# Two layers of a graph network: the gathered half of each node table first, and ScalarE scales the nodes' own part

## The chip, the cores and the metric

One core of a Trainium2 chip. The metric is the device time of one execution in microseconds (us), median of several. The core's engines run their own instruction streams in order and meet through semaphores: TensorE (PE, with PEld for its weight loads), VectorE (DVE), ScalarE (ACT), GpSimd (POOL) and SyncE (SP), which only starts transfers.

## The reference

6,250 nodes of 128 features, 106,250 edges sorted by destination. Two layers, each behind a layer norm and a ReLU, `h`, and each added to `x`:

```python
# layer 0: attention (GATv2)
xl, xr = h @ Wl + bl, h @ Wr + br
logits = leaky_relu(xl[src] + xr[dst] + edge_attr @ We, 0.2) @ att
out    = segment_sum(xl[src] * segment_softmax(logits, dst)[:, None], dst) + bias_out
x      = x + batch_norm(gelu(h + out))
# layer 1: messages, gated
em       = relu(layer_norm(concat(h[src], h[dst]) @ msg_w + msg_b)) * w[:, None]
messages = segment_mean(em, dst)
gate     = sigmoid(h @ gate_w + gate_b)
h_new    = relu(layer_norm(concat(h, messages) @ upd_w + upd_b))
x        = x + gate * h_new + (1 - gate) * h
```

## The kernel before

**Tiles.** A tile `t` is 125 nodes (50 tiles), a group `g` is four tiles (13 groups; the last has two). Edges lie in 64 chunks of 1,664 (13 x 128). A chunk's destinations fall in one or two windows of 125 nodes; a *pair* is a chunk and a window. There are 64 pairs, k = 0 to 63, worked in four blocks b of 4, 3, 3 and 3 tiles of 128 edges.

**Order.** Each layer goes through: layer norm statistics of the nodes, the *table stage*, the pair loop, and an end. The second layer has one more stage between table stage and pair loop, the *own part*.

**Table stage** (`tables` on TensorE and VectorE, `tables_of` on ScalarE). For each group: ScalarE normalises its rows (`norm_rows`, L1020, four instructions), TensorE turns them (`turn_rows`, L707), ScalarE copies them with ReLU into `feat_h` (`features`, L1014), TensorE multiplies each tile with the layer's 256 columns (`project`, L715: columns 0 to 127 give the row that edges gather by source, columns 128 to 255 the row by destination), VectorE adds the bias to either half (`add_bias`, L1321, two instructions: `rows`, a ring of three groups, and `dst_rows`, which stays on the chip). SyncE stores `rows` to `src_table` in DRAM (L493, two transfers a group); VectorE's writing of group g waits until the store of group g - 3 has landed. PSUM holds two groups (`rows_ps`, two banks each). In the first layer VectorE does other work between the groups (statistics, the list of the pairs). After the last group comes `raw_scale`: pair 0 is not gathered from the table, but from the inputs of the layer norm, so that GpSimd has it early; its rows go through norm, turn and product apart (`raw_norm`, `raw_turn`, `raw_features`, `raw_project`, `raw_rows`).

**Pair loop.** GpSimd gathers the 13 x 128 source rows of pair k into one of four buffers (`gather_pair`, L643, 13 indirect transfers). For k = 1 it first waits for the whole table (`tables_stored`). For k >= 4 each block waits until the buffer is free: in the first layer until the sums of pair k - 4 are made (`gat_sums`, L815), in the second until its messages are (`msg_message`, L888 and L892); and pair k waits for its records (`rec`), which SyncE loads in the second layer only after the messages of pair k - 4 (`feed`, L417). The engines work on a pair in a chain of stages with lags; in the second layer ScalarE makes the one-hot matrix (`one_hot`, L1206 and L1209) from `node_id` (L1555, VectorE), ahead of the pair's first product (L888).

**Own part** (second layer). For each group g: TensorE makes `feat_h` times the update's own columns and the gate's column (`update_own`, L936); ScalarE makes the gate (`gate_of`, L1224); VectorE makes `rest` = 1 - gate (L1757), `node_h` = max(node_h, 0) * rest (L1759), `node_x` += `node_h` (L1763), and then takes the product out of PSUM into `node_h` (L1765). PSUM again holds two groups:

```python
            def update_own(g):
                t0, t1 = GROUPS[g]
                pe.wait_ge(s_row, NGX + NG)
                ge(pe, s_zh, g - 1)
```

`s_zh` counts the groups whose L1765 is done, so the product of group g waits for the taking out of group g - 2. TensorE starts the pair loop once all 13 are taken out.

Of the kernel before, what the change touches and what calls it, by code (L numbers as in the profile page):

```python
# [15 lines left out]
D = 128  # L16
# [3 lines left out]
PP = 125  # L20
# [39 lines left out]
def gnn_layers(nc, a, out):  # L60
    with ExitStack() as ctx:
# [176 lines left out]

        rows_ps = [psum[:, (2 + 2 * u) * 512:(4 + 2 * u) * 512].rearrange("p (i f) -> p i f", i=GT) for u in range(2)]
# [41 lines left out]
        s_row = sem("s_row")  # L281
        s_src_out = [sem(f"s_src_out{u}") for u in range(3)]
# [87 lines left out]
        s_held = sem("s_held")  # L370
        s_zh = sem("s_zh")
# [329 lines left out]
        def turn_rows(pe, n, g):  # L701

            t0, t1 = GROUPS[g]
            pe.wait_ge(s_norm, n * NGX + g + 1)
            ge(pe, s_ht, n * NGX + g - 1 if g > 1 else 0)
            for t in range(t0, t1):
                i = nc.tensor.transpose(turn_ps[g % 2][:, t - t0, 0:PP], node_h[:, t, :], ident[0:PP, 0:PP])  # L707
            i.then_inc(s_tr, 1)

        def project(pe, n, g, weights):  # L710
            t0, t1 = GROUPS[g]
            pe.wait_ge(s_ht, n * NGX + g + 1)
            ge(pe, s_row, n * NGX + g - 1 if g > 1 else 0)
            for t in range(t0, t1):
                i = nc.tensor.matmul(rows_ps[g % 2][0:PP, t - t0, :], feat_h[:, t, :], weights[:, :], start=True, stop=True)  # L715
            i.then_inc(s_proj, 1)

# [8 lines left out]
        def tables(pe, n, weights):  # L726
            turn_rows(pe, n, 0)
            for g in range(NG):
                if g + 1 < NG:
                    turn_rows(pe, n, g + 1)  # L730
                project(pe, n, g, weights)
                if n == 0 and g == 6:
                    spread_chunks(pe)

# [7 lines left out]
        def raw_turn(pe, n, b):  # L742

            t0, t1 = BLK[b]
            pe.wait_ge(s_norm, raw_group(n, b) + 1)
# [14 lines left out]
        def _(pe):  # L760
# [170 lines left out]
            def update_own(g):  # L931
                t0, t1 = GROUPS[g]
                pe.wait_ge(s_row, NGX + NG)
# [65 lines left out]
        def _(act):  # L999
# [41 lines left out]
            def tables_of(n):  # L1041
# [7 lines left out]
                for g in range(NG):  # L1049
# [3 lines left out]
                    if ahead <= g + 2 < NG:  # L1053
                        norm_rows(n, g + 2)
# [171 lines left out]

            raw_deviations(1)
            for g in range(NG):
                gate_of(g)
                if g in RAW_NORM:  # L1230
                    raw_norm(1, RAW_NORM.index(g))
                if g in RAW_FEATURES:
                    raw_features(1, RAW_FEATURES.index(g))
            act.wait_ge(s_src_out[2], 2 * 32 * SLOT_GROUPS[2])
# [49 lines left out]
        def _(dve):  # L1284
# [27 lines left out]
            def add_bias(n, g, bias):  # L1312
# [6 lines left out]
                for h, to in enumerate((rows[0:PP, g % 3, 0:nt, :], dst_rows[:, t0:t1, :])):  # L1319
                    f = slice(h * D, (h + 1) * D)  # L1320
                    i = dve.tensor_tensor(to, rows_ps[g % 2][0:PP, 0:nt, f],  # L1321
                                          bias[0:PP, f].unsqueeze(1).to_broadcast([PP, nt, D]), ALU.add)
                i.then_inc(s_row, 1)
# [160 lines left out]
            raw_scale(0, gat)  # L1484
            rest_of_weights(0)
# [262 lines left out]
            layer_norm_scale(1, 1)  # L1748
            tables(1, msg_b, {})
            raw_scale(1, msg)  # L1750


            def own_part(g):
                t0, t1 = GROUPS[g]
                nt = t1 - t0
                dve.wait_ge(s_gate, g + 1)
                dve.tensor_scalar(rest[:, t0:t1], gate[:, t0:t1], -1.0, 1.0, ALU.mult, ALU.add).then_inc(s_rest, 1)  # L1757
                dve.wait_ge(s_rest, g + 1)
                dve.scalar_tensor_tensor(out=node_h[:, t0:t1, :], in0=node_h[:, t0:t1, :], scalar=0.0,  # L1759
                                         in1=rest[:, t0:t1].unsqueeze(2).to_broadcast([PP, nt, D]), op0=ALU.max,  # L1760
                                         op1=ALU.mult).then_inc(s_held, 1)
                dve.wait_ge(s_held, 2 * g + 1)
                dve.tensor_tensor(node_x[:, t0:t1, :], node_x[:, t0:t1, :], node_h[:, t0:t1, :], ALU.add).then_inc(s_held, 1)  # L1763
                dve.wait_ge(s_held, 2 * g + 2)
# [4 lines left out]
            for g in range(NG):  # L1769
                own_part(g)  # L1770
# [164 lines left out]
```

## Time and profile before

| | us |
|---|---|
| median of 3 runs (lowest, highest) | 2270.16 (2269.47, 2271.11) |
| the profiled execution: its time | 2270.79 |
| its span, first to last instruction | 2269.0 |
| busy: PE / PEld | 1644.5 / 1231.5 |
| busy: DVE / ACT / POOL | 1709.5 / 1232.5 / 1634.4 |
| mean granted TensorE clock | 0.902 |
| DMA | 83 GB/s, 189.19 MB |

Busy times are of one profiled execution; its time is 1.8 us more than its span. In the rows below, a timeline merges instructions of one line that follow each other: start in us, length in us, engine and line, what is written <- read, shapes, and how many; in brackets the idle time of the engine before it and what ended it ("issue": nothing that the profile shows). A float32 product is two MATMUL instructions, so a group of four tiles counts x8. A busy engine is not by itself the one that sets the end; which wait ends last in a stage has to be read there.

### The profile page before, as it was taken

To read this page: it belongs to the slowest core of one execution; us is meant where nothing else is said; L and a number is where in the kernel's file an instruction comes from. 1 tells how busy PE (TensorE), PEld (TensorE's weight loads), DVE (VectorE), ACT (ScalarE), POOL (GpSimd) and SP (SyncE) were. 2 spreads that over 40 slices of the span, in tenths; PEclk is the share of its full clock that TensorE was granted. 3 is DMA by queue.
4 is the path that set the end of the run, shared out by engine and by line. 5 is a ranking of instruction groups with operands and counts; after the bars stand their busy time and mean duration, and the time that the engine had idled before them with its cause. 6 is when DMAs were issued, how large, how long until landed. Compare 5 with 4: busy or idle time off the path is not lost.

```text
span 2269.0 us, 43295 instructions
## 1 busy us (share of the span) xinstructions
PE 1644.5 (72%) x9256; PEld 1231.5 (54%) x9256; DVE 1709.5 (75%) x6093; ACT 1232.5 (54%) x3996; POOL 1634.4 (72%) x1742
## 2 busy tenths in 40 slices
PE   5488887777778777877776767767766776666666
PEld 4265555555545555555565555555655655555454
DVE  6787777676777777777768777778778778777777
ACT  5344444444434444444556666667666666566655
POOL 5777777777777777777137777777777777777774
PEclk9799999999999999999978888888888888898988
DMA  9433333333333333332242332332333333323322
GB/s 190 100 86 86 86 78 84 86 77 84 78 86 77 82 81 84 77 83 72 54 114 66 85 83 78 84 84 76 83 84 76 83 85 80 79 76 83 76 68 62
DMA packets 176752, 189.19 MB, mean 83 GB/s; under 512 B 100940, under 2 KB 132708, under 8 KB 176564
## 3 DMA queue, kind: packets, MB, share of 16 engines
q0 software_dynamic: 54192, 111.40, 20.0%
q1 hardware_dynamic: 120965, 75.89, 13.1%
q10 hardware_dynamic: 1472, 0.73, 0.2%
q14 instruction: 103, 0.84, 0.1%
q8 instruction: 20, 0.33, 0.1%
HBM read 172.91 MB, written 14.97 MB: 83 GB/s over the span
## 4 chain that ended last, share of the span: by engine, by line
POOL 31%; issue 18%; PE 14%; DVE 12%; ACT 10%; DMA 3%; DVEq 2%; POOLq 1%; ACTq 0%
POOL room L643 31%; PE psum L888 4%; ACT room L1206 4%; PE psum L892 3%; DVE room L1818 3%; DMA room<-src_table,rec 3%; ACT room L1209 2%; PE psum L815 2%; ACT rows L1186 2%; ACT room L1198 1%; PE psum L715 1%; PE psum L797 1%; DVE room L1804 1%; DVEq L1535 1%; DVE dfar L1561 1%
## 5 line engine op out<-in xcount | busy, mean ns | idle before, releaser
L643 POOL DMA_INDIRECT room<-src_table,rec x1638 | 1564.7, 955 | 519.1 <-issue 482.1
L888 PE MATMUL psum<-room,ident 128*128 128x384 f32 (+1 forms) x512 | 286.0, 645 | 295.7 <-ACT room L1209 207.0
L1186 ACT ACTIVATE rows<-psum 128x128 f32<-128x128 f32 x832 | 216.9, 271 | 318.3 <-DVE room L1804 318.3
L892 PEld LDWEIGHTS psum<-room 125*128 125x128 f32 x1664 | 277.0, 230 | 112.5 <-issue 64.1
L815 PE MATMUL psum<-room 128*125 128x128 f32 x1664 | 255.9, 294 | 85.8 <-ACT room L1136 81.9
L1118 ACT ACTIVATE room<-psum 128x384 f32<-128x384 f32 (+1 forms) x256 | 130.4, 509 | 289.6 <-PE psum L787 281.6
L815 PEld LDWEIGHTS psum<-room 128*125 128x125 f32 x1664 | 210.3, 195 | 136.6 <-ACT room L1136 135.5
L1599 DVE TENSOR_TENSOR room<-psum,room 128x384 f32<-128x384 f32 (+1 forms) x256 | 150.9, 590 | 173.4 <-ACT room L1118 88.5
L892 PE MATMUL psum<-room 125*128 125x128 f32 x1664 | 273.4, 312 | 0.0
L888 PEld LDWEIGHTS psum<-room,ident 128*128 128x128 f32 x512 | 92.1, 225 | 315.2 <-ACT room L1209 167.0
L1804 DVE TENSOR_TENSOR room<-psum,msg_g 128x384 f32<-128x384 f32 (+1 forms) x256 | 150.2, 587 | 149.9 <-PE psum L892 149.9
L905 PE MATMUL psum<-room 128*125 128x128 f32 x1664 | 249.8, 293 | 13.5 <-ACT room L1198 11.9
L1818 DVE SCALAR_TENSOR_TENSOR room<-room,rstd_e,msg_beta 128x128 f32<-128x128 f32 x832 | 244.1, 351 | 10.2
L905 PEld LDWEIGHTS psum<-room 128*125 128x125 f32 x1664 | 226.5, 207 | 20.2 <-issue 16.1
L797 PE MATMUL psum<-room,natt 128*125 128x384 f32 (+1 forms) x512 | 231.4, 535 | 6.3 <-DVE room L1599 6.1
L787 PE MATMUL psum<-ident,room 128*128 128x128 f32 x832 | 143.8, 287 | 118.9 <-DMA room<-src_table,rec 117.8
L1794 DVE TENSOR_SCALAR room<-nfree,rec 128x125 f32<-128x125 f32 x832 | 227.4, 367 | 0.1
L1127 ACT ACTIVATE room<-room,nloc 125x384 f32<-125x384 f32 (+1 forms) x256 | 163.8, 640 | 91.1 <-DVE nloc L1614 88.1
L787 PEld LDWEIGHTS psum<-ident,room 128*128 128x128 f32 x832 | 100.3, 144 | 185.5 <-DMA room<-src_table,rec 170.6
L780 PE MATMUL psum<-room 128*128 128x384 bf16 (+1 forms) x768 | 182.3, 348 | 21.1 <-DVE room L1591 21.1
L1186 ACT ACTIVATION_READ_ACCUMULATOR rows<-psum 128x1 f32 x832 | 168.9, 203 | 0.0
L805 PEld LDWEIGHTS psum<-ident,room 125*128 125x128 f32 x832 | 110.5, 146 | 103.0 <-issue 72.1
(250 smaller groups left out, 2650.6 us busy)
## 6 DMA issues: line engine op xcount, KB each, us to landing
room<-dst_perm SPq DMA_DIRECT2D x128, 416.0 KB
room<-src_table,rec POOLq DMA_INDIRECT x1638
src_table<-rows SPq DMA_DIRECT2D x24, 224.0 KB
node_x<-in_x SPq DMA_DIRECT2D x5, 560.0 KB
x_rows<-node_x SPq DMA_DIRECT2D x12, 224.0 KB
out_rows<-node_x SPq DMA_DIRECT2D x12, 224.0 KB
rec<-rec_rows SPq DMA_DIRECT2D x125, 19.5 KB
pair_info<-pair_list SPq DMA_DIRECT2D x128, 2.0 KB
```

The costliest lines, as they stand in the source:

```text
L643: pool.indirect_dma_start(out=xg[:, u, t * P:(t + 1) * P], out_offset=None, in_=table[:, :], in_offset=bass.IndirectOffsetOnAxis(ap=rec[:, ...
L780: nc.tensor.matmul(m_bank[c][:, cols], dws[:, v, p, :], oht[:, v, t0 * P:t1 * P], start=(p == 0), stop=False, skip_group_check=True)
L787: i = nc.tensor.matmul(m_bank[c][:, j * P:(j + 1) * P], xg[:, u, t * P:(t + 1) * P], ident[:, :], start=False, stop=(t == t1 - 1), is_tran ...
L797: nc.tensor.matmul(logit_bank[c][0:W, cols], natt[:, :], act_m[:, c, cols], start=True, stop=True).then_inc(s.logit, 1)
L815: i = nc.tensor.matmul(sum_bank[u % 2][0:W, 0:D], prob[:, c, t - t0, 0:W], xg[:, u, t * P:(t + 1) * P], start=(t == 0), stop=(t == T - 1), ...
L888: nc.tensor.matmul(msg_bank[b][:, cols], ident[:, :], xg[:, u, t0 * P:t1 * P], start=True, stop=False, skip_group_check=True)
L892: i = nc.tensor.matmul(msg_bank[b][:, j * P:(j + 1) * P], msg_oht[0:W, v, t * P:(t + 1) * P], dwin[0:W, v, :], start=False, stop=(t == t1 ...
L905: i = nc.tensor.matmul(sum_bank[u % 2][0:W, 0:D], pm[:, u % 2, t, 0:W], zr[:, b, j * P:(j + 1) * P], start=(t == 0), stop=(t == T - 1), sk ...
L1186: i = nc.scalar.activation(sq[:, j * P:(j + 1) * P], msg_bank[b][:, j * P:(j + 1) * P], ACT.Square, accum_out=var_e[:, c, j:j + 1])
L1794: i = dve.tensor_scalar(pm[:, v, t, 0:W], nfree[:, v, :], rec[:, u, T + t:T + t + 1], rec[:, u, 2 * T + t:2 * T + t + 1], ALU.is_equal, AL ...
L1804: dve.tensor_tensor(hgs[:, c, 0:nt * P].rearrange("p (j f) -> p j f", f=D), msg_bank[b][:, 0:nt * P].rearrange("p (j f) -> p j f", f=D), m ...
L1818: i = dve.scalar_tensor_tensor(out=xz[:, c, j * P:(j + 1) * P], in0=hgs[:, c, j * P:(j + 1) * P], scalar=rstd_e[:, c, j:j + 1], in1=msg_be ...
```

## The change

*Tables.* The product of a tile is made in two passes of 128 columns. `project` makes the gathered half for all 13 groups first, into four half-size places in PSUM (`half_ps`), and VectorE's `add_bias` writes only `rows`. A new pass over the groups, `project_near` on TensorE and `near_rows` on VectorE, makes `dst_rows`; on VectorE it stands behind `raw_scale`, on TensorE ahead of `raw_turn` (first layer) and of `update_own` (second). In the second layer VectorE normalises groups 9 to 12 (14 instructions) in ScalarE's place.

*Own part.* VectorE's L1759 goes. ScalarE multiplies instead (`kept`, one instruction for each tile, ReLU with `rest` as scale), for group g - 1 right behind the gate of group g. VectorE makes `rest` of group g ahead of the rest of its work on group g - 1.

```diff
         def project(pe, n, g, weights):
             t0, t1 = GROUPS[g]
             pe.wait_ge(s_ht, n * NGX + g + 1)
-            ge(pe, s_row, n * NGX + g - 1 if g > 1 else 0)
+            ge(pe, s_row, n * NGX + g - 3 if g > 3 else 0)
+            if n == 1 and g < 4:
+                pe.wait_ge(s_near_row, NG)
             for t in range(t0, t1):
-                i = nc.tensor.matmul(rows_ps[g % 2][0:PP, t - t0, :], feat_h[:, t, :], weights[:, :], start=True, stop=True)
+                i = nc.tensor.matmul(half_ps[g % 4][0:PP, t - t0, :], feat_h[:, t, :], weights[:, 0:D], start=True, stop=True)
             i.then_inc(s_proj, 1)
+
+        def project_near(pe, n, g, weights):
+            t0, t1 = GROUPS[g]
+            if g < 4:
+                pe.wait_ge(s_row, n * NGX + NG + g - 3)
+            else:
+                pe.wait_ge(s_near_row, n * NG + g - 3)
+            for t in range(t0, t1):
+                i = nc.tensor.matmul(half_ps[(NG + g) % 4][0:PP, t - t0, :], feat_h[:, t, :], weights[:, D:2 * D], start=True, stop=True)
+            i.then_inc(s_near_proj, 1)
...
             def update_own(g):
                 t0, t1 = GROUPS[g]
-                pe.wait_ge(s_row, NGX + NG)
+                pe.wait_ge(s_near_row, 2 * NG)
                 ge(pe, s_zh, g - 1)
...
-                    if ahead <= g + 2 < NG:
+                    if ahead <= g + 2 < NG and (n == 0 or g + 2 not in NORM_DVE):
                         norm_rows(n, g + 2)
...
+            def kept(g):
+                act.wait_ge(s_rest, g + 1)
+                for t in range(*GROUPS[g]):
+                    i = nc.scalar.activation(node_h[:, t, :], node_h[:, t, :], ACT.Relu, scale=rest[:, t:t + 1])
+                i.then_inc(s_kept, 1)
+
             raw_deviations(1)
             for g in range(NG):
                 gate_of(g)
+                if g > 0:
+                    kept(g - 1)
                 if g in RAW_NORM:
                     raw_norm(1, RAW_NORM.index(g))
                 if g in RAW_FEATURES:
                     raw_features(1, RAW_FEATURES.index(g))
+            kept(NG - 1)
...
+            def near_rows(n, bias):
+
+                for g, (t0, t1) in enumerate(GROUPS):
+                    nt = t1 - t0
+                    dve.wait_ge(s_near_proj, n * NG + g + 1)
+                    dve.tensor_tensor(dst_rows[:, t0:t1, :], half_ps[(NG + g) % 4][0:PP, 0:nt, :],
+                                      bias[0:PP, D:2 * D].unsqueeze(1).to_broadcast([PP, nt, D]), ALU.add).then_inc(s_near_row, 1)
...
             layer_norm_scale(1, 1)
+            dve.wait_ge(s_norm_scale, PART0[1] + 2)
+            for g in NORM_DVE:
+                for t in range(*GROUPS[g]):
+                    i = dve.tensor_scalar(node_h[:, t, :], node_x[:, t, :], rstd[:, t:t + 1], nmr[:, t:t + 1], ALU.mult, ALU.add)
+                i.then_inc(s_norm_dve, 1)
             tables(1, msg_b, {})
             raw_scale(1, msg)
+            near_rows(1, msg_b)
...
+            def rest_of(g):
+                t0, t1 = GROUPS[g]
                 dve.wait_ge(s_gate, g + 1)
                 dve.tensor_scalar(rest[:, t0:t1], gate[:, t0:t1], -1.0, 1.0, ALU.mult, ALU.add).then_inc(s_rest, 1)
-                dve.wait_ge(s_rest, g + 1)
-                dve.scalar_tensor_tensor(out=node_h[:, t0:t1, :], in0=node_h[:, t0:t1, :], scalar=0.0,
-                                         in1=rest[:, t0:t1].unsqueeze(2).to_broadcast([PP, nt, D]), op0=ALU.max,
-                                         op1=ALU.mult).then_inc(s_held, 1)
-                dve.wait_ge(s_held, 2 * g + 1)
+
+            def own_part(g):
+                t0, t1 = GROUPS[g]
+                nt = t1 - t0
+                dve.wait_ge(s_kept, g + 1)
                 dve.tensor_tensor(node_x[:, t0:t1, :], node_x[:, t0:t1, :], node_h[:, t0:t1, :], ALU.add).then_inc(s_held, 1)
-                dve.wait_ge(s_held, 2 * g + 2)
+                dve.wait_ge(s_held, g + 1)
                 dve.tensor_tensor(node_h[:, t0:t1, :], rows_ps[g % 2][0:PP, 0:nt, 0:D],
                                   upd_b[0:PP, :].unsqueeze(1).to_broadcast([PP, nt, D]), ALU.add).then_inc(s_zh, 1)
 
             dve.wait_ge(s_x1_out, NG * 32)
-            for g in range(NG):
-                own_part(g)
+            for g in range(NG + 1):
+                if g < NG:
+                    rest_of(g)
+                if g > 0:
+                    own_part(g - 1)
                 if g in RAW_ROWS:
                     raw_rows(1, RAW_ROWS.index(g), msg_b)
```

## Rows read from the trace of the kernel before

**Rows 1.** page, costliest groups: busy us, mean ns, idle before and releaser

```profile
L643 POOL DMA_INDIRECT room<-src_table,rec x1638 | 1564.7, 955 | 519.1 <-issue 482.1
```

**Rows 2.** line 643 from 1250 to 2230 us: idle before it, us and times

```profile
  issue: 226.7, 744
  PE psum L892: 6.7, 22
```

**Rows 3.** line 888 from 1219 to 1900 us: idle before it, us and times

```profile
  DMA room<-src_table,rec: 0.6, 1
```

**Rows 4.** line 888 from 1900 to 2215 us, the same

```profile
  DMA room<-src_table,rec: 100.0, 52
```

**Rows 5.** GpSimd's timeline: start, length (us), line, [idle before <-releaser]

```profile
62.47 3.88 POOL L643 DMA_INDIRECT room<-src_table,rec  x1 [3.31 <-DMA src_table<-rows]
...
115.02 0.94 POOL L643 DMA_INDIRECT room<-src_table,rec  x1 [0.30 <-issue]
...
1181.14 0.94 POOL L643 DMA_INDIRECT room<-src_table,rec  x1 [17.25 <-DMA src_table<-rows]
...
1230.41 0.96 POOL L643 DMA_INDIRECT room<-src_table,rec  x1 [0.30 <-DMA rec<-rec_rows]
...
1234.21 0.94 POOL L643 DMA_INDIRECT room<-src_table,rec  x1 [0.30 <-issue]
```

**Rows 6.** TensorE's timeline at the first pairs of either layer

```profile
112.50 1.14 PE L815 MATMUL psum<-room 128*125 128x128 f32 x8 [0.78 <-ACT room L1136]
...
1219.29 2.07 PE L888 MATMUL psum<-room,ident 128*128 128x512 f32 x2 [7.80 <-ACT room L1209]
```

**Rows 7.** SyncE's timeline: the records of pairs 4 and 5, second layer

```profile
1228.22 0.39 SPq L417 DMA_DIRECT2D rec<-rec_rows  x1
...
1244.94 0.38 SPq L417 DMA_DIRECT2D rec<-rec_rows  x1
```

**Rows 8.** VectorE's timeline in the first layer's tables

```profile
33.99 0.69 DVE L1321 TENSOR_TENSOR rows<-psum,b_lr 125x512 f32<-125x512 f32 x1 [3.49 <-DMA src_table<-rows]
34.60 0.68 DVE L1321 TENSOR_TENSOR dst_rows<-psum,b_lr 125x512 f32<-125x512 f32 x1
...
57.06 0.41 DVE L1321 TENSOR_TENSOR rows<-psum,b_lr 125x256 f32<-125x256 f32 x1
...
61.82 0.17 DVE L1341 SCALAR_TENSOR_TENSOR raw_nmr<-raw_nmr,raw_rstd 128x13 f32<-128x13 f32 x1
```

**Rows 9.** timelines, second layer's tables: ScalarE, TensorE, VectorE

```profile
1155.49 1.64 ACT L1020 ACTIVATE node_h<-node_x,nmr,rstd 125x128 f32<-125x128 f32 x4
...
1159.13 1.89 PE L715 MATMUL psum<-msg_wc,feat_room 128*125 128x256 f32 x8
...
1177.16 0.41 DVE L1321 TENSOR_TENSOR rows<-psum,msg_b 125x256 f32<-125x256 f32 x1
```

**Rows 10.** timelines in the own-part stage, TensorE, ScalarE, VectorE

```profile
1188.04 2.05 PE L936 MATMUL psum<-upd_w,feat_room 128*125 128x129 f32 x8 [0.20 <-DVE node_h L1765]
...
1192.93 1.12 PE L936 MATMUL psum<-upd_w,feat_room 128*125 128x129 f32 x8 [1.15 <-DVE node_h L1765]
...
1190.13 0.26 ACT L1224 ACTIVATE gate<-psum,gate_b 125x4 f32<-125x4 f32 x1 [1.99 <-PE psum L936]
...
1192.89 0.69 DVE L1759 SCALAR_TENSOR_TENSOR node_h<-node_h,rest 125x512 f32<-125x512 f32 x1
1193.62 0.69 DVE L1763 TENSOR_TENSOR node_x<-node_x,node_h 125x512 f32<-125x512 f32 x1
1194.34 0.69 DVE L1765 TENSOR_TENSOR node_h<-psum,upd_b 125x512 f32<-125x512 f32 x1
...
1214.93 0.16 DVE L1555 TENSOR_TENSOR node_id<-turned,iota_p 128x1 f32<-128x1 f32 x1
```

**Rows 11.** stretches: busy us (count) by engine, granted clock, DMA share, GB/s

```profile
1183.00:1190.00 7.00, 4.02 (x17) 3.78 (x18) 6.12 (x12) 2.13 (x7) 5.48 (x6) 0.56 0.18 45
1190.00:1200.00 10.00, 7.56 (x60) 6.91 (x59) 9.59 (x18) 5.62 (x16) 7.87 (x8) 0.97 0.16 44
```

More of the change, by code:

```diff
@@ L237, in z_bank @@
             return banks[2 + g % NZ][0:PP, :].rearrange("p (i f) -> p i f", i=GT)
+        half_ps = [banks[2 + u].rearrange("p (i f) -> p i f", i=GT) for u in range(4)]
         rows_ps = [psum[:, (2 + 2 * u) * 512:(4 + 2 * u) * 512].rearrange("p (i f) -> p i f", i=GT) for u in range(2)]
@@ L281, in gnn_layers @@
         s_row = sem("s_row")
+        s_near_proj = sem("s_near_proj")
+        s_near_row = sem("s_near_row")
+        s_norm_dve = sem("s_norm_dve")
+        NORM_DVE = (9, 10, 11, 12)
         s_src_out = [sem(f"s_src_out{u}") for u in range(3)]
@@ L703, in turn_rows @@
             t0, t1 = GROUPS[g]
-            pe.wait_ge(s_norm, n * NGX + g + 1)
+            if n == 1 and g in NORM_DVE:
+                pe.wait_ge(s_norm_dve, NORM_DVE.index(g) + 1)
+            else:
+                pe.wait_ge(s_norm, n * NGX + g + 1)
             ge(pe, s_ht, n * NGX + g - 1 if g > 1 else 0)
@@ L733, in tables @@
                     spread_chunks(pe)
+            for g in range(NG):
+                project_near(pe, n, g, weights)
         RAW_NORM, RAW_TURN, RAW_FEATURES, RAW_PROJECT, RAW_ROWS = (range(i, i + 2 * NB, 2) for i in (1, 3, 4, 5, 6))
@@ L744, in raw_turn @@
             t0, t1 = BLK[b]
-            pe.wait_ge(s_norm, raw_group(n, b) + 1)
+            pe.wait_ge(s_norm, raw_group(n, b) + 1 - (len(NORM_DVE) if n == 1 else 0))
             for t in range(t0, t1):
@@ L1318, in add_bias @@
                 ge(dve, s_src_out[g % 3], 32 * (n * SLOT_GROUPS[g % 3] + g // 3))
[L1319 to L1323, printed above, removed]
+                dve.tensor_tensor(rows[0:PP, g % 3, 0:nt, :], half_ps[g % 4][0:PP, 0:nt, :],
+                                  bias[0:PP, 0:D].unsqueeze(1).to_broadcast([PP, nt, D]), ALU.add).then_inc(s_row, 1)
+            def near_rows(n, bias):
[4 more added lines that the diff above has]
+                                      bias[0:PP, D:2 * D].unsqueeze(1).to_broadcast([PP, nt, D]), ALU.add).then_inc(s_near_row, 1)
             def raw_scale(n, s):
@@ L1748, in _ @@
             layer_norm_scale(1, 1)
+            dve.wait_ge(s_norm_scale, PART0[1] + 2)
[3 more added lines that the diff above has]
+                i.then_inc(s_norm_dve, 1)
             tables(1, msg_b, {})
             raw_scale(1, msg)
+            near_rows(1, msg_b)
+            def rest_of(g):
+                t0, t1 = GROUPS[g]
+                dve.wait_ge(s_gate, g + 1)
+                dve.tensor_scalar(rest[:, t0:t1], gate[:, t0:t1], -1.0, 1.0, ALU.mult, ALU.add).then_inc(s_rest, 1)
             def own_part(g):
```

5 lines of the change are left out of this document (3 added, 2 removed).

## Prediction, made before the changed kernel ran

> **What bounds the kernel now.** I read the page's costliest groups first. GpSimd's gathers [rows 1] take 955 ns each and stand 0.3 us apart, so 13 of them, one pair, take 16.3 us, and 63 pairs fill 1,025 us of each layer. The waits of that line [rows 2] then show that in the second layer's loop it waits for nothing but its own issue: 226.7 us in 744 waits are issue, 6.7 us in 22 end with TensorE, at the same 0.3 us each. So in both loops the gathers are one unbroken run, and the end comes as much later as the gathers of pair 4 and later come later. Whether the engines or GpSimd lead has to be asked apart. TensorE's first product of a block waits 0.6 us for gathered rows up to 1900 us, and 100.0 us after it [rows 3, 4]: in the second layer the engines start far behind the gathers, catch up about 1 us a pair and then live on them. A late start of the engines therefore counts only through what it does to GpSimd, if it is made up by the end.
>
> Next come GpSimd's timeline and what releases it [rows 5 to 7]. Pairs 1 to 3 need the stored table: the run starts at 62.47 and at 1181.14. Pair 4 is the 40th gather, at 115.02 and at 1234.21, and needs a buffer or records that only the engines' work on pair 0 frees. In the first layer TensorE's first sums of pair 0 end at 112.50 + 1.14 = 113.64; the gather comes at 115.02, so the slack is 1.3 us. In the second the records of pair 4 are asked for at 1228.22, after pair 0's messages, and have landed by 1230.41 (2.2 us): slack 3.8 us. Those of pair 5, asked for at 1244.94, land at 1247.1, and its gather is due 16.4 us after 1234.21, at 1250.6: slack 3.5 us. Thus a table stored earlier gives at most these slacks, 1.3 and 3.5 us, and a start of the engines later than they allow is paid in full.
>
> **Tables, first layer.** VectorE's two halves of a group stand at 33.99 and 34.60 [rows 8]: 0.6 us each, so taking out 12.5 of them spares 7.5 us before the last table row. Not all of it comes through: the row of 33.99 waited 3.49 us for the store of three groups earlier to land. Such landings stay where they are while the transfers of the opening run, and a faster VectorE only waits longer. I take 1.8 us of the 7.5 (bounds 0 and 7.5). The table is then stored some 2.7 us sooner, which pair 1 gets. The half rows come back behind `raw_scale`, in front of everything that VectorE still does before pair 0. VectorE alone would need 7.5 us. TensorE must make them too, out of four places: four groups are ready, the fifth can start when the first is taken out. A product of eight instructions of 128 columns takes 1.14 us, about 0.98 us from one to the next [rows 6]; after a pause it takes 2.05 [rows 10]. That is 0.6 + 8 x 0.98 + 0.5 + 0.4 = 9.3 us, or 11.4 with two slow groups; I take 10.4. From the last row to the end of `raw_scale`, 57.06 to 61.99, 0.3 us of the other half goes. So pair 0 starts 10.4 - 1.8 - 0.3 = 8.3 us later, its first sums end at 121.9, and the gather of pair 4 moves from 115.02 to 122.0: **+7.0 us** (likely 4 to 9; bounds -1.3, if all 7.5 us come through and TensorE keeps up, and +10).
>
> **Tables, second layer.** Before, ScalarE's four norms of a group take 1.64 us and a copy about 0.5, and TensorE's 256 columns 1.89 with a turn beside them [rows 9]: a group about every 2.1 us from either. Now TensorE needs 0.98 and about 0.43 for the turn, and ScalarE has norms for four groups fewer. VectorE's 14 norms, at most 0.38 us each, lie in its wait for the first products. The last row, at 1177.16 before, I put at 1170.3 (VectorE writes one half at 0.6 us; stores of three groups need to land within 4.2 us). `raw_scale` takes 4.3 us, then the other half 9.4 us with TensorE quick: 1184.0. The first gate is ready at 1184.1 + 1.12 + 0.3 = 1185.5.
>
> **Own part.** Here the order of waits matters more than the work. Before, a group cost VectorE three instructions about 0.7 us apart (1192.89, 1193.62, 1194.34) and a short one, some 2.25 us, with everything else beside it; ScalarE waited 1.99 us before a gate [rows 10]. Now ScalarE's stream reads: gate of g, multiplication of g - 1, gate of g + 1. The gate of g + 1 needs TensorE's product, which needs a free half of PSUM, which needs VectorE's taking out of g - 1, which needs the multiplication of g - 1 that has only just ended. No step of this ring overlaps another, although two groups fit in PSUM. One turn [rows 9, 10]: gate to multiplication 0.16; four instructions 1.64; to VectorE 0.06; addition 0.73; taking out 0.69; to TensorE 0.15; product 1.12, or 2.05 at the lower clock; to ScalarE 0.04. Sum 4.59 or 5.52 us. The product is slow where the granted clock averages 0.56 and quick where it is 0.97 [rows 11]; TensorE was busy 4.02 of 7 us in the one and 7.56 of 10 in the other. In the ring it works 1.1 to 2.0 us a turn, and as much again in every second turn on pair 0's rows, so it will be now on one level, now on the other: 5.1 us.
>
> The first multiplication ends at 1188.1, eleven turns later it is 1244.2; the half group, VectorE's last two takings out and the node numbers bring `node_id` to 1247.3, against 1215.09. The engines start pair 0 **32.2 us** later (26.6 to 36.9 by the two levels). Of pair 0's raw rows, ScalarE's norms and copies, TensorE's turns and products and VectorE's additions lie in the ring's waits and cost nothing. What the removed L1759 gives, 13 x 0.7 = 9 us of VectorE, is worth nothing, for VectorE waits in the ring.
>
> SyncE is queued behind it: the records of pair 4 are asked for after pair 0's messages. So GpSimd, done with pairs 1 to 3 some 53 us after its start near 1173.5, stands idle from about 1227 to 1263. With the slack of pair 5 the run moves by 32.2 - 3.5 = **+28.7 us** (23.1 to 33.4). The engines' own lag grows by only 3.5 us, which at 1 us a pair is made up before the last 15 pairs.
>
> **Sum.** 7.0 + 28.7 = 35.7 us on a span of 2269.0 gives 2304.7; its own time 2270.79 becomes 2306.5. The median lies 0.6 below that time: 2306.
>
> **Two rules.** ScalarE's four instructions take 1.64 us [rows 9], 410 ns each. The Trainium skill (VectorE: DVE Perf Modes, the section on the TRN2 errata) gives ScalarE 224 cycles and one a column at 1.2 GHz, and says that many small tiles pay the fixed part each time; 50 instructions where VectorE had 13 are what it warns of. Its figure is 293 ns; by it, as an estimate, a turn is 0.47 us shorter and the sum 2301. The trace's row decides here.
>
> The quick and slow product are the rows' two levels, 2.4 and 1.2 GHz. The Trainium skill (TensorE: Matmul & The Clock Gate, What's actually happening) calls the lower one the default that activity lifts; taken at its word, a TensorE busy a quarter to a third of each turn stays low, a turn is 5.52 us and the sum about 2311. That TensorE is on the lower level throughout is the last case below.
>
> **Rivals.**
> *The ring isn't closed; ScalarE is the bound.* If the multiplication of g - 1 were covered by a product already made, ScalarE's work would count: 13 gates of 0.16, 50 x 0.41, 13 x 0.41 for the raw norms, 2 us of copies: 30 us from 1185.5, `node_id` at about 1217.5. That is 2.4 us later, inside the slack of 3.5; only the first layer's 7.0 is left: 2276. ScalarE's 1.99 us waits speak for room; `update_own`'s unchanged wait speaks against it.
> *Faster: the start of the gathers decides.* If VectorE's relief (0.7 of 2.25 us a group) shortened the own part, to node numbers before 1215, GpSimd would gain up to the 3.5 us of the second layer, and with the first layer's halves hidden 1.3 there: 2266. It decides from a turn under 2.2 us and under 1.3 us of added wait before pair 0. Against it stand the ring and a VectorE with no pause between `raw_scale` and pair 0.
> *TensorE on the lower level throughout.* Turns of 5.52 us add 4.7; nearly all second-half groups at 2.05 us delay the own part by a further 9: 2320. For it speaks TensorE's short share of a turn; against it 0.97 in a stretch with waits of 1.15 us.
>
> **How the numbers follow.** Forecast 0.84, ScalarE bound 0.06, faster 0.04, lower level throughout 0.06. The forecast's own range is 2297 to 2315, from 4 and 23.1 up to 9 and 33.4 with a little for pair 0's start. It holds some nine tenths of its case; half of the slow case and the forecast's edges bring the range 2293 to 2319 to 8 in 10. About 0.2%, 4.5 us, is what a measurement of this kernel can tell from no change. Within it falls a part of the second case: 0.02; faster 0.04; slower 0.94.
>
> **What would show it.** Gates (L1224) about 5 us apart, each of ScalarE's waits ended by L936 and each of VectorE's by ScalarE's multiplication. GpSimd idle some 37 us before pair 4 of the second layer, the wait ended by the records, and 7 us before pair 4 of the first, ended by L815. The table stored earlier in both layers, about 2.7 and 7 us. Gates 2.3 to 2.6 us apart would make me wrong; so would gathers of pair 4 that don't follow the engines.

## The result and the profile after

The changed kernel takes **2309.8 us** (median of 4, 2307.9 to 2310.6), the kernel before 2270.4 beside it: ratio 1.0171 (1.0159 to 1.0183), 1.7% slower. Forecast were 2306 and a range of 2293 to 2319. The profiled execution has a span of 2308.8 us, 39.8 more than before, at a mean granted clock of 0.893.

The gathers' line of the page, and GpSimd's timeline at the points of [rows 1, 5]:

```profile
L649 POOL DMA_INDIRECT room<-src_table,rec x1638 | 1559.5, 952 | 570.6 <-issue 480.0
```

```profile
61.77 0.99 POOL L649 DMA_INDIRECT room<-src_table,rec  x1 [10.01 <-DMA src_table<-rows]
...
125.38 0.94 POOL L649 DMA_INDIRECT room<-src_table,rec  x1 [7.73 <-PE psum L838]
...
1183.75 0.94 POOL L649 DMA_INDIRECT room<-src_table,rec  x1 [8.39 <-DMA src_table<-rows]
...
1271.96 0.94 POOL L649 DMA_INDIRECT room<-src_table,rec  x1 [39.44 <-DMA rec<-rec_rows]
...
1290.82 1.07 POOL L649 DMA_INDIRECT room<-src_table,rec  x1 [2.93 <-DMA rec<-rec_rows]
```

The idle time before the gathers grew by 51.5 us in all; the part put down to issue did not grow (482.1 us before, 480.0 now). Two waits that [rows 5] don't have set the time: 7.73 us ahead of pair 4 in the first layer, ended by TensorE's sums, and 39.44 in the second, ended by the records. Pair 4 moved from 115.02 to 125.38, **+10.4 us**, and from 1234.21 to 1271.96; the last gather of the kernel starts 39.8 us later than before. So the second layer has **+29.5**. Its table is stored at 1183.75, 7.8 us sooner within the layer (1181.14 + 10.4 - 1183.75), and that gains nothing: GpSimd only waits longer ahead of pair 4.

Behind the two waits, TensorE's and SyncE's timelines (they answer to [rows 6, 7]):

```profile
123.46 1.14 PE L838 MATMUL psum<-room 128*125 128x128 f32 x8 [0.78 <-ACT room L1159]
...
1260.77 2.07 PE L911 MATMUL psum<-room,ident 128*128 128x512 f32 x2 [9.05 <-ACT room L1232]
```

```profile
1269.13 0.39 SPq L423 DMA_DIRECT2D rec<-rec_rows  x1
...
1287.51 0.38 SPq L423 DMA_DIRECT2D rec<-rec_rows  x1
```

The sums come 10.96 us later, the records of pair 4 are asked for 40.9 us later. VectorE's timeline in the first layer's tables ([rows 8]); L1351 writes table rows, L1359 the near rows:

```profile
34.16 0.69 DVE L1351 TENSOR_TENSOR rows<-psum,b_lr 125x512 f32<-125x512 f32 x1 [3.17 <-DMA src_table<-rows]
...
49.07 0.69 DVE L1351 TENSOR_TENSOR rows<-psum,b_lr 125x512 f32<-125x512 f32 x1 [4.32 <-DMA src_table<-rows]
...
58.30 0.43 DVE L1351 TENSOR_TENSOR rows<-psum,b_lr 125x256 f32<-125x256 f32 x1 [1.71 <-DMA src_table<-rows]
...
62.75 0.17 DVE L1378 SCALAR_TENSOR_TENSOR raw_nmr<-raw_nmr,raw_rstd 128x13 f32<-128x13 f32 x1
62.84 2.48 DVE L1359 TENSOR_TENSOR dst_rows<-psum,b_lr 125x512 f32<-125x512 f32 x4
...
72.50 1.02 DVE L1359 TENSOR_TENSOR dst_rows<-psum,b_lr 125x512 f32<-125x512 f32 x2 [0.18 <-PE psum L736]
```

The view by tile says how long VectorE waited, from 20 to 66 us, before it could write `rows` (us, times). In the trace of the kernel before this line reads 5.5, 3:

```profile
  DMA src_table<-rows: 13.3, 5
```

VectorE was relieved of 7.5 us between the table's rows and waited 7.8 us more for stores to land. The last row is written at 58.30, no sooner than before (57.06). Then the near rows take 10.7 us, with TensorE the slower of the two at the end (0.18 us before each).

One turn of the own part, all engines but GpSimd and the transfers ([rows 10]):

```profile
1207.54 0.26 ACT L1247 ACTIVATE gate<-psum,gate_b 125x4 f32<-125x4 f32 x1 [3.69 <-PE psum L959]
1207.70 1.27 ACT L1253 ACTIVATE node_h<-node_h,rest 125x128 f32<-125x128 f32 x4
1207.83 0.17 DVE L1800 TENSOR_SCALAR rest<-gate 125x4 f32<-125x4 f32 x1 [2.54 <-ACT gate L1247]
...
1209.00 0.69 DVE L1806 TENSOR_TENSOR node_x<-node_x,node_h 125x512 f32<-125x512 f32 x1 [0.99 <-ACT node_h L1253]
1209.72 0.69 DVE L1808 TENSOR_TENSOR node_h<-psum,upd_b 125x512 f32<-125x512 f32 x1
...
1210.56 2.05 PE L959 MATMUL psum<-upd_w,feat_room 128*125 128x129 f32 x8 [2.21 <-DVE node_h L1808]
1212.65 0.26 ACT L1247 ACTIVATE gate<-psum,gate_b 125x4 f32<-125x4 f32 x1 [2.54 <-PE psum L959]
```

The ring is there as the prediction drew it: gate, multiplication, addition, taking out, product, gate, each released by the one before, 5.11 us a turn. All 13 gates together waited 43.9 us for the product (the view of line 1247), and TensorE's granted clock over these turns (window, columns as in [rows 11]) was nearly at the lower level:

```profile
  PE psum L959: 43.9, 13
```

```profile
1200.00:1250.00 50.00, 27.93 (x119) 25.25 (x119) 17.02 (x34) 19.58 (x64) 24.90 (x26) 0.54 0.14 36
```

### The profile page after: what moved, and what is told of

Its sections match the earlier page's. It is cut to its first block, busy times and chain, and to the rows that moved or that the text cites. A ratio compares the mean times of both kernels' runs of the same rounds, so it can differ in the third digit from the quotient of the medians.

```text
span 2308.8 us, 43732 instructions
## 1 busy us (share of the span) xinstructions
PE 1661.4 (72%) x9456; PEld 1259.5 (55%) x9456; DVE 1709.2 (74%) x6094; ACT 1240.4 (54%) x4032; POOL 1629.2 (71%) x1742
## 4 chain that ended last, share of the span: by engine, by line
POOL 32%; issue 19%; PE 14%; DVE 12%; ACT 10%; DMA 3%; DVEq 2%; POOLq 1%; ACTq 0%; SPq 0%
POOL room L649 32%; PE psum L911 4%; ACT room L1229 3%; PE psum L915 3%; DVE room L1864 3%; DMA room<-src_table,rec 3%; PE psum L838 2%; ACT room L1232 2%; ACT rows L1209 1%; PE psum L820 1%; PE psum L959 1%; PE psum L810 1%; DVEq L1573 1%; ACT room L1221 1%; DVE room L1850 1%
## 5 line engine op out<-in xcount | busy, mean ns | idle before, releaser
L649 POOL DMA_INDIRECT room<-src_table,rec x1638 | 1559.5, 952 | 570.6 <-issue 480.0
```

What stands on the lines that cost most here:

```text
L649: pool.indirect_dma_start(out=xg[:, u, t * P:(t + 1) * P], out_offset=None, in_=table[:, :], in_offset=bass.IndirectOffsetOnAxis(ap=rec[:, ...
```

## The experiments

The first four kernels ran on one chip beside the kernel before, which took 2271.0 us there. In each experiment's diff, `...` stands for lines left out.

**One half of the change each.** `tables_only` has the changed table stages and the own part of before. Its diff against the changed kernel:

```diff
             for g in range(NG):
                 gate_of(g)
-                if g > 0:
-                    kept(g - 1)
...
-                dve.wait_ge(s_kept, g + 1)
+                dve.wait_ge(s_gate, g + 1)
+                dve.tensor_scalar(rest[:, t0:t1], gate[:, t0:t1], -1.0, 1.0, ALU.mult, ALU.add).then_inc(s_rest, 1)
+                dve.wait_ge(s_rest, g + 1)
+                dve.scalar_tensor_tensor(out=node_h[:, t0:t1, :], in0=node_h[:, t0:t1, :], scalar=0.0,
+                                         in1=rest[:, t0:t1].unsqueeze(2).to_broadcast([PP, nt, D]), op0=ALU.max,
+                                         op1=ALU.mult).then_inc(s_held, 1)
+                dve.wait_ge(s_held, 2 * g + 1)
...
```

> The changed table stages in both layers with the own part of before. If the ring in the own part is what costs the second layer 29 us: pair 4 of the first layer stays where the changed kernel has it (125.4 us, 10.4 later than before), the own part takes 31 to 32 us from its first gate again, and of the second layer's delay only 0 to 1.5 us is left: a span of 2279 to 2281. If instead the second layer's added wait before the own part (near rows behind the scale) is itself a large part of the 29 us, the span is 2285 or more. If the earlier table of the second layer is worth something by itself, the span is 2276 or less.

`own_only` is the kernel before with `rest_of`, `kept` and the shorter `own_part` of the change.

> The table stages of before with the own part as changed. The ring theory: gates 5.1 us apart, node numbers about 27 us later than before (1242), gathers of pair 4 and 5 of the second layer 24 to 26 us later, pair 4 of the first layer at 115.0 as before, a span of 2293 to 2296. The rival, that ring and tables only cost so much together (TensorE left cold by the tables, for instance), puts the turn under 4.5 us and the span under 2290.

Measured: tables only 2278.7 us, ratio 1.0031 (1.0020 to 1.0042); own part only 2298.6, ratio 1.0119 (1.0102 to 1.0136). Thus +7.7 and +27.6, together 35.3 of the 39.4 that the whole costs. The tables' span, 2277.9 us, is 1.1 below what was expected, and that of the own part, 2298.1, is 2.1 above; gates stand 5.11 us apart with the own part alone, so the ring needs no help from the tables. Pair 4's gather in the second layer, with the tables alone (L649) and with the own part alone (L644):

```profile
1241.08 0.94 POOL L649 DMA_INDIRECT room<-src_table,rec  x1 [6.06 <-DMA rec<-rec_rows]
```

```profile
1259.34 0.95 POOL L644 DMA_INDIRECT room<-src_table,rec  x1 [27.66 <-DMA rec<-rec_rows]
```

With the tables alone, pair 4 of the first layer is 8.6 us late, and within the second layer it is 1.7 us *early*. That does not last: pair 5 then waits 2.92 us for its own records and starts 9.4 us late (1259.99), so that 0.9 us of the delay is the second layer's. With the own part alone the first layer is as before, and the wait in the second is ended by the same records.

**Opening the ring by order alone.** The changed kernel with two pairs of calls exchanged, so that ScalarE's multiplication of g - 1 stands ahead of the gate of g, and VectorE's addition and taking out of g - 1 ahead of `rest` of g. No work changes.

```diff
             for g in range(NG):
-                gate_of(g)
                 if g > 0:
                     kept(g - 1)
+                gate_of(g)
...
-                if g < NG:
-                    rest_of(g)
                 if g > 0:
                     own_part(g - 1)
+                if g < NG:
+                    rest_of(g)
```

> The changed kernel with the same instructions in another order: ScalarE multiplies group g - 1 ahead of the gate of g, and VectorE finishes group g - 1 ahead of the subtraction of g. If the closed ring is the cost, a turn falls from 5.11 to about 3.0 us (addition 0.73, taking out 0.69, subtraction 0.27, multiplication 1.26 and the ways between), node numbers come about 17 us earlier, at 1239, and the span is about 2292 (2289 to 2296). If the amount of ScalarE's work or the fixed part of its 50 instructions is the cost, nothing moves: 2307 to 2310.

Measured 2284.0 us, ratio 1.0056 (1.0039 to 1.0073): 25.9 us faster than the changed kernel. Its span, 2282.7 us, lies 6.3 below the expected range. Its timeline:

```profile
1207.34 1.28 ACT L1253 ACTIVATE node_h<-node_h,rest 125x128 f32<-125x128 f32 x4 [0.77 <-DVE rest L1800]
1207.37 1.11 PE L959 MATMUL psum<-upd_w,feat_room 128*125 128x129 f32 x8 [1.59 <-DVE node_h L1808]
...
1208.53 0.26 ACT L1247 ACTIVATE gate<-psum,gate_b 125x4 f32<-125x4 f32 x1
1208.65 0.69 DVE L1806 TENSOR_TENSOR node_x<-node_x,node_h 125x512 f32<-125x512 f32 x1 [1.35 <-ACT node_h L1253]
...
1209.37 0.69 DVE L1808 TENSOR_TENSOR node_h<-psum,upd_b 125x512 f32<-125x512 f32 x1
1209.98 0.17 DVE L1800 TENSOR_SCALAR rest<-gate 125x4 f32<-125x4 f32 x1
1210.18 1.28 ACT L1253 ACTIVATE node_h<-node_h,rest 125x128 f32<-125x128 f32 x4 [0.24 <-DVE rest L1800]
```

Product and gate have left the ring: they start and end beside the multiplication. What is left is multiplication, addition, taking out, `rest`: 2.85 us a turn, still above the 2.25 of before [rows 10]. A quick product alone can't account for this gain: `filler`, the next run, has it in the closed ring and gains 10.8 us. The order of the calls was the large price. That of the multiplications' new place is small: this kernel is 5.3 us slower than the one with the changed tables alone. The expectation had the turn nearly right, at 3.0 us, and its sum wrong: twelve turns that are 2.1 us shorter make 25 us, not 17. The node numbers are ready at 1232.24, 24.2 us sooner than in the changed kernel; 2.4 of these are the first layer's, whose pair 4 starts at 122.95.

**The clock's part.** The changed kernel with dummy products in the turns of groups 1 to 11 (nine a turn, or four where TensorE has pair 0's raw product to make), into a free bank, so that TensorE doesn't rest in the ring:

```diff
+                if 0 < g < NG - 1:
+                    for _ in range(4 if g in RAW_PROJECT else 9):
+                        nc.tensor.matmul(banks[7 if g < 8 else 0][0:PP, 0:D], feat_h[:, g, :], upd_w[:, 0:D], start=True, stop=True)
```

> The changed kernel with products that nobody reads behind each group's product in the own part (nine tiles, four where pair 0's rows are made), into banks that are free then: they only keep TensorE busy in its wait. If the lower clock is the 0.94 us by which the turn stands above 4.2 us, the product takes 1.1 in place of 2.06 us in about ten turns and the span falls by 8 to 11 us, to about 2299. If the clock does not follow TensorE's own load, the product stays at 2.06 us and the span at 2308 or above.

Measured 2299.0 us, ratio 1.0124 (1.0107 to 1.0141). More work for TensorE took 10.8 us off. In its window the granted clock is 1.00 for 0.54, TensorE is busy 30.4 of 40 us for 27.9 of 50, and the product takes 1.11 us; gates stand 4.18 us apart in place of 5.11:

```profile
1200.00:1240.00 40.00, 30.38 (x258) 28.73 (x256) 16.04 (x32) 19.33 (x63) 27.54 (x27) 1.00 0.18 46
```

```profile
1212.14 1.11 PE L959 MATMUL psum<-upd_w,feat_room 128*125 128x129 f32 x8 [1.09 <-DVE node_h L1811]
...
1213.29 0.26 ACT L1250 ACTIVATE gate<-psum,gate_b 125x4 f32<-125x4 f32 x1 [2.27 <-PE psum L959]
```

The last gather starts 11.6 us sooner than in the changed kernel. Some 9.7 of these are the own part (node numbers at 1246.73 for 1256.41); about as much as is left, 1.7, is that the records of pair 5 are asked for 16.7 us after those of pair 4 and not 18.4.

**The tables of the second layer alone**, all else as before (a kernel beside it ran 2271.0, as for the next three):

> The tables of the second layer alone are built as the change builds them; the first layer's tables and the whole own part stay as before. The run with both layers' tables changed and the own part as before came out 7.7 us over the kernel before, and the fourth pair's gather of its first layer 8.6 us later. Theory A: all of that is the first layer's, where the near rows (10.6 us) stand on the path; in the second layer the messages' node rows are asked for some 2.8 us later, which the slack of about 3.5 us hides, and the earlier table store is hidden as well: 2270 to 2272 us, the same. Theory B: the near rows cost in the second layer too: 2273 us or more. Theory C: the table stored 7.6 us sooner lets GpSimd start sooner and that reaches the end: 2265 us or less.

Measured 2270.6 us, ratio 1.0000 (0.9991 to 1.0009): theory A. The 7.7 us of `tables_only` are the first layer's, to within the 1 us or so that a median can tell. The node numbers are ready some 2.4 us later within the layer, which is hidden; the table stored 6.1 us sooner within the layer gains nothing either.

**A fourth buffer for the table's rows.** The changed kernel with `rows` and its semaphores four deep:

```diff
-        rows = sb("rows", [P, 3, GT, D])
+        rows = sb("rows", [P, 4, GT, D])
...
-                ge(dve, s_src_out[g % 3], 32 * (n * SLOT_GROUPS[g % 3] + g // 3))
+                ge(dve, s_src_out[g % 4], 32 * (n * SLOT_GROUPS[g % 4] + g // 4))
...
```

> The changed kernel with four buffers for the table rows in place of three (and one semaphore fewer elsewhere). VectorE's 13.3 us of waits for stored rows in the first layer should fall to under half. Theory A (the waits for landings took what the removed near rows gave): the last row of the table is written some 4 to 6 us sooner, the near rows follow, and the time falls by as much: 2304 to 2307 us. Theory B (the stores themselves are the limit, and the wait moves on to them): the table is stored no sooner, but the near rows still start earlier, because VectorE runs ahead of the stores by one group more: 2306 to 2308 us. Theory C (the near rows don't stand on the path): 2309 to 2311 us.

Measured 2302.9 us, ratio 1.0135 (1.0120 to 1.0150), 6.9 less than the changed kernel. Lines by tile and by GpSimd's timeline:

```profile
  DMA src_table<-rows: 9.1, 5
```

```profile
119.56 0.95 POOL L648 DMA_INDIRECT room<-src_table,rec  x1 [7.37 <-PE psum L837]
```

The last row is written at 52.93 (58.30 with three buffers) and pair 4 starts 5.8 us sooner: theory A, 1.1 us below its range. Landings had taken what the removed near rows gave, and the fourth buffer does not give all of it back. The wait did not fall under half: two thirds of it remained. And beside the kernel before with four buffers (`before_four`, below), whose last row stands at 53.96 and whose VectorE never waits for a landing there, the near rows taken from between bring the last row 1.0 us forward, not 7.5.

**Putting the multiplication elsewhere.** If VectorE shall be relieved in the own part, the multiplication and the addition can be one instruction a tile there. ScalarE's norms already end in a ReLU, so the maximum can go. On the kernel before:

```diff
-                dve.scalar_tensor_tensor(out=node_h[:, t0:t1, :], in0=node_h[:, t0:t1, :], scalar=0.0,
-                                         in1=rest[:, t0:t1].unsqueeze(2).to_broadcast([PP, nt, D]), op0=ALU.max,
-                                         op1=ALU.mult).then_inc(s_held, 1)
-                dve.wait_ge(s_held, 2 * g + 1)
-                dve.tensor_tensor(node_x[:, t0:t1, :], node_x[:, t0:t1, :], node_h[:, t0:t1, :], ALU.add).then_inc(s_held, 1)
+                for t in range(t0, t1):
+                    i = dve.scalar_tensor_tensor(out=node_x[:, t, :], in0=node_h[:, t, :], scalar=rest[:, t:t + 1],
+                                                 in1=node_x[:, t, :], op0=ALU.mult, op1=ALU.add)
+                i.then_inc(s_held, 1)
...
```

First with the second layer's tables as changed (the four groups that VectorE normalises there get their ReLU by an instruction of their own), and then with two groups of its near rows moved up between far ones:

> The second layer's tables as in the change, the first layer as before, and the own part wholly on VectorE, with the multiplication by one less the gate and the addition of the nodes in one instruction per column tile (node_h * rest + node_x), no maximum, and the ReLU of VectorE's four norms put between the rows of the table. A group of the own part should take about 1.95 us on VectorE in place of 2.25, over 12.5 groups 3.8 us less; the nodes' rows are then asked for about 1 us sooner than before the change. Theory A: 2265 to 2268 us. Theory B (the path in the second layer is not VectorE's but the table's store and the gathers): 2269 to 2272 us.

> As the kernel with the fused own part, but the near rows of the first two groups are written between the far rows of groups 5, 6 and after, so that 1.4 us less of them stands behind the table. Theory A: 1 to 2 us faster than that kernel, 2263 to 2267 us. Theory B (the waits for stored rows take the room): the same as that kernel within 1 us.

Measured 2268.3 us for either, ratios 0.9984 (0.9975 to 0.9992) and 0.9987 (0.9978 to 0.9995): the first is 0.3 us above its theory A, and the moved near rows gave nothing that shows, its theory B. Then by itself, and with the fourth buffer (before beside these three: 2270.0):

> The kernel before with only the own part fused on VectorE (node_h * rest + node_x in one instruction per column tile; the maximum goes). A group should take some 0.3 us less, 3.8 us over the second layer. Theory A (in the kernel before, the store of the second layer's table holds GpSimd as long as the node side does): 2269.5 to 2271.5 us, the same, and the fused own part needs the table stored sooner to be worth anything. Theory B (the node side holds it): 2266 to 2268 us.

> The kernel before the change with four buffers for the table rows in place of three. Its VectorE waits 5.5 us in the first layer for stored rows; in the changed kernel the fourth buffer took 4.2 us off such waits (13.3 to 9.1) and 6.9 us off the time. Theory A (landings hold the first layer back here too, if less): 1.5 to 4 us faster, 2267 to 2269.5 us. Theory B (here VectorE's near rows fill the waits, so nothing is gained): 2270 to 2272 us.

> The kernel with the second layer's tables of the change, the fused own part on VectorE and the first two near rows between far rows (2268.3 us), with four buffers for the table rows. Theory A (the gain of the fourth buffer is the first layer's and adds to it): 2264 to 2267 us, below both kernels by 0.2% or more. Theory B: no further gain, 2268 to 2270 us.

Measured: fused own part alone 2267.0 (0.9983, 0.9974 to 0.9992), fourth buffer alone 2266.7 (0.9983, 0.9974 to 0.9992; VectorE's 5.5 us of waits for stores in the first layer are gone), all together **2259.4** (0.9951, 0.9937 to 0.9964), 0.5% faster than the kernel before and 2.2% faster than the changed one. The first fits its theory B by its number, the second is 0.3 us below its theory A. The third is 4.6 us faster than its theory A: the fourth buffer, expected to help the first layer alone, takes 3.2 us off there (pair 4 at 111.07 for 114.31 in `second_fused_two`), and in the second layer's tables a last wait of 1.5 us for a landing goes and the node numbers come 2.2 us sooner within the layer.

The fused own part gained 3 us where theory A of its expectation said nothing, and not for theory B's reason either. GpSimd's timeline in that kernel:

```profile
1182.54 0.94 POOL L643 DMA_INDIRECT room<-src_table,rec  x1 [16.77 <-DMA src_table<-rows]
...
1231.47 0.94 POOL L643 DMA_INDIRECT room<-src_table,rec  x1 [0.30 <-issue]
```

Pair 4 follows pair 3 without a wait, as before [rows 5]: the node side did not hold it. But the 39 gathers of pairs 1 to 3 took 48.9 us, and 53.1 before (1181.14 to 1234.21). The last section shows where they gained it.

**The fused own part and the fourth buffer, without any part of the change.**

> The kernel before with the fused own part and four buffers for the table rows, and no part of the change. Each alone measured 0.9983 of the kernel before (2267.0 and 2266.7 us against 2270.0); the kernel that has both, and the second layer's tables of the change too, measured 0.9951 (2259.4 us). Theory A (GpSimd's start is then the limit of the second layer, and only the table stored first makes use of the faster own part): the two gains don't add up, 2263.5 to 2267 us. Theory B (the second layer's tables as changed give nothing): 2258 to 2261 us.

Measured 2262.7 us, ratio 0.9963 (0.9949 to 0.9977; before 2271.3). It lies beneath theory A's range by 0.8 us and above theory B's by 1.7, so it decides for neither; its interval overlaps that of the kernel that has the second layer's tables too (0.9937 to 0.9964). Their traces differ: here pair 4 starts at 1227.42 right behind pair 3, there at 1223.18 after a wait for records, and the last gathers start at 2207.46 and 2203.32. Two lines of the kernel with those tables:

```profile
1170.16 0.94 POOL L648 DMA_INDIRECT room<-src_table,rec  x1 [9.41 <-DMA src_table<-rows]
...
1223.18 0.99 POOL L648 DMA_INDIRECT room<-src_table,rec  x1 [4.29 <-DMA rec<-rec_rows]
```

Whether the second layer's tables are worth these 3 to 4 us once both sides of the own part are faster stays open at this precision.

## Why the prediction was right

**The mechanism** held in its main steps: the two waits, what ended them, the ring, GpSimd's idle time (39.4 and 7.7 us; said were some 37 and 7), and in the second layer a table that is stored sooner for nothing. Sizes in it did not, as the terms below show. `order` shows that the cause of the large term is the closed ring: with the same instructions, 25.9 us go. The three rivals fall. ScalarE as the bound wants gates that wait for nothing, and they waited 43.9 us. A faster end wants turns under 2.2 us. The lower clock level was nearly true of the ring, but its 2320 needs two more things that did not come: slow near rows (from 1190 to 1200 us the granted clock was 1.00) and multiplications of 1.64 us.

**The sum** was 35.7 us for a measured 39.8 of span, each term by itself:

*First layer, +7.0 forecast, +10.4 in the trace after* (+10.3 in `filler`, +8.6 in `tables_only`, +7.9 in `order`, which have the same tables). The near rows took 10.7 us for 10.4. What failed is "I take 1.8 us of the 7.5": of VectorE's relief nothing came through here, -1.2 us; in the other three traces the last row stands at 57.2, 55.5 and 56.1, which is -0.2, 1.5 and 1.0 us. The waits for landings and the `four_buffers` run show that the stores took most of it. In the trace after, the first layer's table is stored 0.7 us sooner and not 2.7. The lower bound, 0 of 7.5, was nearer to their mean than the 1.8. The slack of 1.3 us was mis-sized as well: the gather of pair 4 started 0.78 us after the sums had ended (124.60 to 125.38), and pair 0's 10.96 us became 10.36, so 0.6 us of slack was there.

*Turn of the ring, 5.1 us forecast, 5.11 measured.* This is luck: two errors that cancel. The four multiplications were priced by the norms, 1.64 us [rows 9], and took 1.26; one alone is 0.39 us, so the step from one to the next is (1.26 - 0.39) / 3 = 0.29 us. The 293 ns that the prediction drew from the Trainium skill (VectorE: DVE Perf Modes, the section on the TRN2 errata) was the right one, and the row of the norms the wrong neighbour: those read a scale and a bias per partition, these a scale only (which of these makes the difference was not tried). And the product was taken as now quick, now slow; from 1200 on it took 2.05 or 2.06 us in nine of ten full groups and 1.11 in one, whose turn is 4.17 us. `filler` puts the price on the second: 0.94 us a turn. With the right multiplication and the mixed clock a turn would have been 0.38 us shorter and the sum some 4.6 us less, about 2301, too low. The Trainium skill's rule on the clock (TensorE: Matmul & The Clock Gate, What's actually happening), taken at its word, had the right level for the ring, and this trace agrees there: 0.54 in the window above.

*Start of the ring.* The last table row was put at 1170.3 and stands at 1179.87, which is 1169.5 once the first layer's 10.4 us are taken off. `raw_scale` follows as said. The near rows of this layer were put at 9.4 and took 10.7, with two slow steps (1.01 and 0.55 us of waits for TensorE). The node numbers come 31 us late for a forecast 32.2.

*Slack, 3.5 us forecast, 1.6 found.* 31.1 us of the engines became 29.5 of GpSimd. The records of pair 5 were asked for 18.4 us after those of pair 4 and not 16.7 [rows 7], which takes 1.7 us of the slack. All fourteen traces have one of the two values: eight have 18.4 us and a granted clock of 0.72 between the requests (the change, `own_only`, `tables_only` and `tables_second` among them), six have 16.7 us and 0.79 or 0.80 (the kernel before and `filler` among them). What decides between the two was not tried. With the right slack the forecast of this layer would have been 30.6 and not 28.7 for a measured 29.5: the engines' delay was put 1.1 us too long and the slack 1.9 us too long, and these two cancel in part.

*Why the halves add up to 4.1 us less than the whole.* Most of this gap is not in the traces: the last gather of the kernel is 9.6 us late with the tables alone and 29.0 with the own part alone, together 38.6 of 39.8. A reason for a gap can be given but is not shown. `tables_second` costs nothing, since its 2.4 us of delay lie inside the slack; in the whole change the own part has used the slack up, and pair 5 of the second layer is 2.4 us later within its layer than in `own_only` (29.9 for 27.5), but at the last gather only 0.4 of these are left. The prediction added the two delays before it took the slack off once.

*What L1759 gives.* "Worth nothing" holds for the changed kernel, whose VectorE waits in the ring. In the kernel before, one instruction a tile for the multiplication and the addition gives 3 us, for a reason that the prediction did not have (last section).

## What to carry to other kernels

When an operation moves to another engine, write down both engines' streams and follow one group around: here the same instructions, with two pairs of calls exchanged, are 26 us apart, and the operation's own duration is the small term. Work taken from between two instructions is worth only what the next wait there leaves over, so ask what else that wait is for (here stores that have to land) and whether another buffer is what was really wanted. A slack hides a delay only once: add the delays of all edits before you take it off.

## What the runs showed of the hardware that was not expected

**GpSimd's gathers are slowed beside VectorE's addition in the own part.** GpSimd's timeline in the kernel before, to be read beside VectorE's in [rows 10]:

```profile
1190.91 1.23 POOL L643 DMA_INDIRECT room<-src_table,rec  x1 [0.31 <-issue]
1192.45 0.94 POOL L643 DMA_INDIRECT room<-src_table,rec  x1 [0.30 <-issue]
1193.69 1.43 POOL L643 DMA_INDIRECT room<-src_table,rec  x1 [0.30 <-issue]
1195.43 1.24 POOL L643 DMA_INDIRECT room<-src_table,rec  x1 [0.30 <-issue]
```

The gather at 1193.69 runs beside L1763 (`node_x` += `node_h`, 1193.62), the one at 1192.45 beside L1765, which reads PSUM, and L1759. Of the 21 gathers from 1183 to 1214 us, 14 overlap an L1763 by 0.1 us and more; they take 1.25 us in the mean (0.94 to 1.43), the other seven 0.94 to 0.95, though six of these overlap L1759. In `tables_second`, with the same own part, it is 1.23 to 1.43 us for all 12 that overlap the addition. In the fused own part, where the addition is a `scalar_tensor_tensor` on 128 columns with a scalar per partition, the 19 gathers that overlap it from 1183 to 1213 us take 0.96 us in the mean, 1.07 at most. That is where 53.1 us for 39 gathers became 48.9. It explains too why a fused own part pays in the kernel before, whose pair 4 starts when pair 3's gathers are through: pair 4's records lay ready for 3.8 us, and the slowing of the gathers, 4.1 us, was about as long.

`own_only` has no L1759, but the same addition (L1772 there, at 1185.52 and 1190.63), and its gathers are slowed all the same:

```profile
1185.62 1.41 POOL L644 DMA_INDIRECT room<-src_table,rec  x1 [0.30 <-issue]
...
1191.07 1.07 POOL L644 DMA_INDIRECT room<-src_table,rec  x1 [0.30 <-issue]
```

The first overlaps the addition by 0.60 us, the second by 0.25. Gathers that only meet its start with their last 0.13 us or so keep their 0.94 to 0.95. That the whole-group addition with both sources in SBUF is the cause is read from overlaps in these four traces; no run changed it alone.

**More work made the engine that was waited for quicker.** In `filler`, four or nine products a turn whose results nobody reads took the granted clock of the ring's turns from 0.54 to 1.00 and the product from 2.05 to 1.11 us; the whole kernel became 10.8 us faster.
